# Key products of a linear-attention block on alternating halves of the array, and context products two tiles behind

## What is computed

```python
q, k, v = heads(x @ Wq), heads(x @ Wk), heads(x @ Wv)
def feature(data, proj, is_query):                 # proj: 266 x 64
    data_dash = (64 ** -0.25 * data) @ proj.T
    diag = (data * data).sum(-1) * 0.5 * 64 ** -0.5
    stab = max over features if is_query else max over everything
    return 266 ** -0.5 * (exp(data_dash - diag - stab) + 1e-4)
qp, kp = feature(q, proj, True), feature(k, proj, False)
context = einsum('nm,ne->me', kp, v)               # per head, with the sums of kp
out = (qp @ context) / (qp @ kp.sum(0))
x = x + out @ Wo + bo
```

## Time and profile before

| | |
|---|---|
| runs shown | 2225.18, 2227.09, 2228.19 us |
| median | 2227.09 us |
| the profiled execution | 2207.3 us |
| its span, first to last instruction | 2205.5 us |
| granted TensorE clock, mean over the span | 0.884 |
| TensorE busy (PE) | 1880.0 us, 85% |
| VectorE (DVE), ScalarE (ACT), GpSimd (POOL) | 1262.1, 469.0, 783.4 us |

### The profile page before, as it was taken

One profiled execution on the slowest core, in us unless ns is written; L12 is line 12 of the kernel. 1 busy time (PEld: TensorE's weight loads), 2 busy tenths in 40 slices (PEclk: granted clock), 3 DMA queues, 4 the chain that ended last, 5 costly groups with the idle time before them and its releaser, 6 DMA issues. The chain is left out here.

```text
span 2205.5 us, 22464 instructions
## 1 busy us (share of the span) xinstructions
PE 1880.0 (85%) x7734; PEld 1200.1 (54%) x7771; DVE 1262.1 (57%) x2841; ACT 469.0 (21%) x995; POOL 783.4 (36%) x688
## 2 busy tenths in 40 slices
PE   4799897777756999979969999799994999888866
PEld 4444445344442444444468887446473888765553
DVE  8666343999967999970114333426243374477523
ACT  4300214111100111111032222222112234344320
POOL 0676772666615677732021221004026101122100
PEclk8799998677767999999959999999997998977888
DMA  5232202766614666650010110101002000000002
GB/s 121 47 86 67 66 5 79 210 194 194 194 36 121 181 184 182 185 159 13 0 58 20 39 39 1 53 2 42 10 1 66 1 1 20 1 1 1 1 1 70
DMA packets 87925, 151.63 MB, mean 69 GB/s; under 512 B 37291, under 2 KB 42565, under 8 KB 87697
## 3 DMA queue, kind: packets, MB, share of 16 engines
q0 software_dynamic: 33280, 93.44, 16.3%
q1 hardware_dynamic: 54545, 56.92, 8.0%
HBM read 131.11 MB, written 19.03 MB: 68 GB/s over the span
## 5 line engine op out<-in xcount | busy, mean ns | idle before, releaser
L1110 POOL DMA_INDIRECT s_vbuf<-v_dram,s_recs x176 | 205.2, 1166 | 144.1 <-DVE s_vw L1138 74.7
L881 POOL DMA_INDIRECT s_kbuf<-k_dram,s_recs x176 | 167.3, 951 | 113.9 <-DVE s_prod L930 42.8
L1163 PE MATMUL s_pV<-s_vw,s_ohf 128*128 128x512 f32 x352 | 195.8, 638 | 0.0
L382 POOL DMA_INDIRECT rec_dram<-s_rec,s_rowid x96 | 115.7, 1205 | 93.0 <-issue 93.0
L953 PE MATMUL s_psQ<-s_qh,s_ohT 128*128 128x512 f32 x176 | 107.5, 611 | 43.4 <-DVE s_prod L930 33.1
L1157 PE MATMUL s_pA<-s_ohd,s_ohb 128*128 128x512 bf16 (+1 forms) x491 | 117.0, 343 | 7.5 <-DVE s_ohf L1136 5.1
L1138 DVE TENSOR_TENSOR s_vw<-s_vbuf,s_W 128x512 f32<-128x512 f32 x176 | 120.3, 683 | 1.7 <-DMA s_vbuf<-v_dram,s_recs 1.7
L1157 PEld LDWEIGHTS s_pA<-s_ohd,s_ohb 128*128 128x128 bf16 x528 | 50.2, 98 | 126.7 <-DVE s_ohf L1136 59.8
L1341 POOL CAST s_wh<-s_w 128x2048 fp32r<-128x2048 f32 x8 | 15.8, 1977 | 281.7 <-PE s_bank L163 157.8
L930 DVE TENSOR_TENSOR s_prod<-s_psQ,s_kbuf 128x512 f32<-128x512 f32 x176 | 112.7, 680 | 1.8 <-PE s_psQ L954 1.2
L936 DVE TENSOR_REDUCE s_W<-s_prod 128x8 f32<-128x512 f32 x176 | 111.5, 673 | 0.0
(11 more groups left out here) (423 smaller groups left out, 4212.2 us busy)
## 6 DMA issues: line engine op xcount, KB each, us to landing
s_w<-in_L_ffn_W SPq DMA_DIRECT2D x16, 512.0 KB
AT_dram<-s_A SPq DMA_DIRECT2D x10, 640.0 KB, 4.6
s_w<-in_L_mix_WqkvT SPq DMA_DIRECT2D x3, 1024.0 KB, 7.7
s_kbuf<-k_dram,s_recs POOLq DMA_INDIRECT x176, 3.8
s_vbuf<-v_dram,s_recs POOLq DMA_INDIRECT x176, 3.7
rec_dram<-s_rec,s_rowid POOLq DMA_INDIRECT x160
k_dram<-s_xn_rows SPq DMA_DIRECT2D x10, 256.0 KB, 2.2
v_dram<-s_xn_rows SPq DMA_DIRECT2D x10, 256.0 KB, 2.1
```

Source lines behind the costliest of these rows:

```text
L382: nc.gpsimd.indirect_dma_start(out=b.rec_dram, out_offset=bass.IndirectOffsetOnAxis(ap=rowid[:, t:t + 1], axis=0), in_=rec[:, t, :], in_of ...
L881: nc.gpsimd.indirect_dma_start(out=kbuf[t % KB][:, :], out_offset=None, in_=b.k_dram, in_offset=bass.IndirectOffsetOnAxis(ap=recs[:, t, 2: ...
L1110: nc.gpsimd.indirect_dma_start(out=vbuf[t % VB][:, :], out_offset=None, in_=b.v_dram, in_offset=bass.IndirectOffsetOnAxis(ap=recs[:, t, 2: ...
L1163: nc.tensor.matmul(V[:, :], ohf[i][:, :], vw[i][:, :], start=False, stop=False, skip_group_check=True).then_inc(used[i], 1)
```

## The change

The key products of two heads are made together: `dash_pair` gives head `h` partitions 0 to 63 of the array and head `h + 1` partitions 64 to 127, in turn, each with 64 rows of `kh`, `kl`, `ph`, `pl` and into a bank of its own; one semaphore increment of 2 tells of both. The maximum uses six banks instead of four. In the context passes the context matmuls of tile `t - 2` follow the key products of tile `t`; `ef` and `el` get a third buffer (`eq[n % 3]`, `el[n % 3]`, in the region of `sq`), `eh` keeps two and VectorE now waits for `used` before it overwrites one. The wait for the copied sums moves from the head of the second half to its third step. The query side is as it was.

```diff
--- before.py
+++ after.py
@@ -1698,6 +1698,7 @@
         sb("sq_reg", [P, 4 * M])
         sq = [b.over("sq_reg", f"sq{i}", [P, D], F32, i * D) for i in range(2)]
         eq = ef + [b.over("sq_reg", "ef2", [P, 4, M])]
+        el.append(b.over("sq_reg", "el2", [P, 4, M], F32R))
         diag = sb("diag", [P, 2, NT, H])
         kmax, kb, qmax, qb, den, rd = (sb(n, [P, NT, H]) for n in ("kmax", "kb", "qmax", "qb", "den", "rd"))
         g1 = sb("g1", [P, 4])
@@ -1759,6 +1760,14 @@
             c, cols = h // 2, slice(t * P, (t + 1) * P)
             return product3(nc, dst, [kh[:, c, cols]], [kl[:, c, cols]], [ph[:, h % 2, :]], [pl[:, h % 2, :]])
 
+        def dash_pair(nc, dsts, t, h):
+            c, cols = h // 2, slice(t * P, (t + 1) * P)
+            for n, (x, y) in enumerate(((kh, ph), (kl, ph), (kh, pl))):
+                for i, dst in enumerate(dsts):
+                    half = slice(i * HD, (i + 1) * HD)
+                    last = nc.tensor.matmul(dst[:, 0:M], x[half, c, cols], y[half, i, :], start=(n == 0), stop=(n == 2))
+            return last
+
         @block.tensor
         def _(pe):
             fs = Filler(pe, bank[0:4], s.fs, s.fs_free)
@@ -1796,11 +1805,11 @@
             pe.wait_ge(s.pl, 1)
             pe.wait_ge(s.kin, 1)
             pe.wait_ge(s.fs_free, fs.n)
-            km = Filler(pe, bank[0:4], s.km, s.km_free)
-            for t in range(NT):
-                for h in range(H):
-                    dst = km.take()
-                    km.done(dash3(nc, dst[:, 0:M], t, h))
+            km = Filler(pe, bank[0:6], s.km, s.km_free)
+            for t in range(NT):
+                for h in range(0, H, 2):
+                    dsts = [km.take(), km.take()]
+                    dash_pair(nc, dsts, t, h).then_inc(s.km, 2)
             pe.wait_ge(s.ones_in, 1)
             gx = Filler(pe, bank[7:8], s.gx, s.gx_free)
             pe.wait_ge(s.dg_free, 1)
@@ -1815,18 +1824,18 @@
 
             ek = Filler(pe, bank[0:4], s.ek, s.ek_free)
             for r in range(2):
-                if r:
-                    pe.wait_ge(s.ctx_in, 4)
-                for t in range(NT + 1):
+                for t in range(NT + 2):
                     if t < NT:
-                        for h in range(4):
-                            dst = ek.take()
-                            ek.done(dash3(nc, dst[:, 0:M], t, 4 * r + h))
-                    if t:
-                        u, n = t - 1, r * NT + t - 1
+                        for h in range(0, 4, 2):
+                            dsts = [ek.take(), ek.take()]
+                            dash_pair(nc, dsts, t, 4 * r + h).then_inc(s.ek, 2)
+                    if r and t == 2:
+                        pe.wait_ge(s.ctx_in, 4)
+                    if t >= 2:
+                        u, n = t - 2, r * NT + t - 2
                         pe.wait_ge(s.ekl, n + 1)
                         for h in range(4):
-                            for i, (x, y) in enumerate(((vh, eh[n % 2]), (vl, eh[n % 2]), (vh, el[n % 2]))):
+                            for i, (x, y) in enumerate(((vh, eh[n % 2]), (vl, eh[n % 2]), (vh, el[n % 3]))):
                                 last = nc.tensor.matmul(bank[4 + h][:VW, 0:M], x[:valid(u), u, 4 * r + h, :], y[:valid(u), h, :],
                                                         start=(u == 0 and i == 0), stop=(u == NT - 1 and i == 2),
                                                         skip_group_check=True)
@@ -1917,11 +1926,11 @@
             for r in range(2):
                 for t in range(NT):
                     n = r * NT + t
-                    if n >= 2:
-                        act.wait_ge(s.used, n - 1)
+                    if n >= 3:
+                        act.wait_ge(s.used, n - 2)
                     for h in range(4):
                         src = ek.take()
-                        ek.done(f(ef[n % 2][:valid(t), h, :], src[:valid(t), 0:M], ACT.Exp, bias=kb[:valid(t), t, 4 * r + h:4 * r + h + 1]))
+                        ek.done(f(eq[n % 3][:valid(t), h, :], src[:valid(t), 0:M], ACT.Exp, bias=kb[:valid(t), t, 4 * r + h:4 * r + h + 1]))
                 act.wait_ge(s.used, (r + 1) * NT)
                 for h in range(4):
                     f(cT[:VW, 4 * r + h, :], bank[4 + h][:VW, 0:M], ACT.Copy).then_inc(s.ctx_in, 1)
@@ -1990,7 +1999,7 @@
                 dve.wait_ge(s.dg_free, i)
 
             transposed(1, s.kin)
-            km = Emptier(dve, bank[0:4], s.km, s.km_free)
+            km = Emptier(dve, bank[0:6], s.km, s.km_free)
             for t in range(NT):
                 for h in range(H):
                     src = km.take()
@@ -2009,9 +2018,11 @@
             for n in range(2 * NT):
                 w = valid(n % NT)
                 dve.wait_ge(s.ek_free, 4 * n + 4)
-                v.tensor_scalar_add(eh[n % 2][:w, :, :], ef[n % 2][:w, :, :], EPS).then_inc(s.ekh, 1)
+                if n >= 2:
+                    dve.wait_ge(s.used, n - 1)
+                v.tensor_scalar_add(eh[n % 2][:w, :, :], eq[n % 3][:w, :, :], EPS).then_inc(s.ekh, 1)
                 dve.wait_ge(s.ekh, n + 1)
-                v.scalar_tensor_tensor(out=el[n % 2][:w, :, :], in0=ef[n % 2][:w, :, :], scalar=EPS,
+                v.scalar_tensor_tensor(out=el[n % 3][:w, :, :], in0=eq[n % 3][:w, :, :], scalar=EPS,
                                        in1=eh[n % 2][:w, :, :], op0=ALU.add, op1=ALU.subtract).then_inc(s.ekl, 1)
             ct = Emptier(dve, bank[0:3], s.ct_half, s.ct_free)
             for i, (_, cw) in enumerate(MC):
```

## The result

The changed kernel takes 2218.74 us, the median of 20 runs (2214.84 to 2227.08); the kernel before, 20 runs beside it, 2226.83 (2220.02 to 2231.18). The ratio is 0.9967, 95% interval 0.9957 to 0.9977: faster by a third of a per cent, about 7.4 us (5.1 to 9.6; the two medians alone lie 8.1 apart). Forecast were 2218 us, and faster by over 0.2% as the likeliest.

What follows compares the result with a forecast made beforehand. TensorE was taken to bound the maximum and both context passes, with VectorE a close second in the maximum. Maximum -1, passes -10 and clock +2 gave -9 us, carried to the median: 2218 us, range 2212 to 2228.5.

Steps and rivals of the forecast that it cites:

- The pair: Key products, maximum and passes: two matmuls on different halves run at the same time, 0.1225 us a pair, now 0.245.
- rival of queueing loads: Key products: weight loads queue, 0.216 us a pair; -1.5 us in all, 2225.6 us; chance 0.25.
- part overlap: Key products: the halves overlap partly, 0.16 us a pair; about -5.3 us, 2221.8 us; chance 0.13.
- no overlap: Key products: loads hidden but halves not simultaneous, 0.245 us a pair; +1.4 us, 2228.5 us; chance 0.08.
- exposed loads: Key products: loads no longer hidden, 0.46 us a pair; about +49 us, 2276 us; chance 0.04.
- Changes of mode: Context tiles: switching the array between halves and whole costs 0.205 and 0.15 us, 0.36 a tile; bounds 0 and 0.8.
- 80 x (0.367 - 0.354): Maximum: 80 heads go from 0.367 us to VectorE's reduction floor of 0.354, -1.0 us; bounds 0 and -1.5.
- Six banks: Maximum: two banks more only let TensorE run ahead of VectorE and bring nothing more.
- The context passes: Both passes, context two tiles behind: a tile takes 2.57 us against 2.95, together 57.2 against 67.7, taken as -10.
- Fill 5.7 as now: Start of the first half: stays 5.7 us, set by table load, exponentials and split; three key-product groups (2.2) fit inside.
- The clock: Context passes' fill and the turn: TensorE may run at 1.2 GHz there, +2 us in all, bounds 0 and +7.
- under 1.00 in the maximum: Sign to look for: a granted clock below 1.00 (2.4 GHz) in the maximum, where TensorE works 0.37 of each 0.71 us.

Runs made afterwards that it cites:

- kept_busy: Changed kernel plus matmuls of no use wherever TensorE starves (maximum, before exchange, fill, turn): 2196.70 us against 2206.46 for the kernel before.
- four_banks: Changed kernel with four banks for the maximum instead of six: 2218.57 us (one run) against 2233.53 (one run) for the kernel before.
- continuous_early: Changed kernel with both halves in one loop, tile 0's key products before the exchange, exponential table loaded early: 2210.73 us against 2225.34 for the kernel before.
- pieces_in_blocks: Changed kernel with one head's three matmuls, then the other's, instead of in turn: 2216.92 us (one run) against 2233.53 (one run) for the kernel before.

## Why the prediction was right

Its total was right, and the mechanism; some of its sizes were not, and that the total comes within 1 us is in part luck: the maximum gained 1.0 more than forecast, the passes 0.9 less, and exchange and clock cost 1.0 more. To compare them each term is taken against the profile of before on which it was made, the passes at a granted clock of 1.00 from kept_busy:

| term | forecast | measured | from |
|---|---|---|---|
| maximum | -1.0 | -2.0 | 28.99 to 27.0 |
| exchange | 0 | +0.2 | 2.27 to 2.47 |
| context passes, clock at 1.00 | -10 | -9.1 | 67.43 to 58.34 |
| clock | +2 | +2.8 | 58.34 to 61.12 |
| sum | -9 | -8.1 | 99.41 to 91.33 |

**The pair.** 0.1225 was called "an assumption all the same, and most of the risk". In the steady tile above two matmuls of a pair start 2 to 7 ns apart, their loads 3 to 9, and pairs 0.12. The Trainium skill, "TensorE: Matmul & The Clock Gate", Part 3 (Packing small matmuls), says that matmuls on different row groups start about 4 ns apart, and this trace agrees. The rival of queueing loads is refuted, and with it part overlap, no overlap and exposed loads.

**Changes of mode.** 0.36 a tile, 0.205 and 0.15; measured 0.34 by doubling them, and 0.19 and 0.14 from the starts in a steady tile.

**The maximum** was mis-sized at the term "80 x (0.367 - 0.354)". DVE was the bound, as forecast, but the floor of a reduction is 0.342. The 0.08 by which two instructions of L936 overlap isn't the overlap of these; two reductions of 0.434 overlap by 0.092. The first reductions of L1997 in the trace of before would have told it (0.345 a step); the whole of the earlier trace rows has PE's waits in it.

**Six banks** "let PE run ahead of DVE and bring nothing more": wrong. The prediction costed the PE side by its rate alone and not by the banks that a pair holds. four_banks puts them at 4.4 us of the maximum. It didn't show in the total because the change has the six.

**The context passes.** Context two tiles behind is in time, by the waits: two of them for `el`, 0.69 each where 0.8 was taken. "Fill 5.7 as now" was 6.2 in kept_busy (1785.71 to 1791.91), where `el` of tile 0 is done after 5.7 as forecast. Three groups of key products don't fit inside at will: the second and third wait for banks that ScalarE frees, and context 0 stands behind them in PE's list; here the last pair starts at 1791.14. Two useless matmuls stand behind it (1791.58), so 6.2 is an upper bound. The turn was 5.4 in the changed kernel, in part at the lower clock, forecast 5.1.

**The clock** cost what was forecast, and in the fill and at the turn, as forecast. Wrong was the sign "under 1.00 in the maximum": there it stayed at 1.00, and fell at 1806.5, behind it. kept_busy gives 2.8 as its price in the passes, within the bounds of 0 and 7; the exchange's 0.2 is gone there too (2.27), so it is 3.0 of the stretch.

**The median.** The 19.8 us "which the trace doesn't explain" are the edge scores: the stage takes 244.6 us in that profile, and 267.0 in the changed kernel's, which is one of the runs timed beside before's 2226.83. That the profile came from another chip than the timed runs is likely, but not on record. To carry microseconds or a percentage to the median gives the same here.

Not shown: why the timed gain of the stretch's later microseconds (kept_busy, continuous_early) doesn't arrive. The stage behind it varies by more than they are worth, and no run held it fixed.

## What to carry to other kernels

Where a contraction fills half of the rows, give two of them one half each; but expect the gain only once whatever consumes the products is moved far enough behind, since TensorE gets ahead of the split that it waits for. A pair takes and returns two banks at once, so count banks before pairing. And where TensorE's work in a stage becomes shorter than that of its neighbour engine, TensorE starves, and here the next stage began at the lower clock. Look at such holes before shaving matmuls: here closing the turn between the passes brought 4.1 us of the stretch, the paired matmuls 3.7.

## What the runs showed of the hardware

- Two halves of the array with 64 rows each run at full speed together, weight loads of 128 columns included: in the maximum a pair's loads start about 30 ns apart, in steady tiles the matmuls 2 to 7.
- The halves don't keep the order of the list between them: matmuls three apart in it started 9 to 14 ns apart (pieces_in_blocks).
- A change from the whole array to halves and back costs 0.34 us, by two changes more a tile; in the starts of one tile 0.19 is the way to the halves and 0.14 the way back.
- The lower clock follows the starved stage: it stayed at 1.00 while PE was busy 1.72 of 3.50 us at the end of the maximum (1803.0 to 1806.5), and was 0.50 in the 10.2 us behind it. The seven profiles with pairs in the maximum and none of the added or early work have the same 10.2 us, beginning 0.6 to 1.2 us behind the last reduction; kept_busy has none.
- The kernel before shows such stretches too, 3.4 and 6.8 us, in one profile of two, though PE is busy all through its maximum. Why only in one isn't shown.
- Reductions of 128 x 266 from PSUM, recorded with 0.434 us, follow each other every 0.342 when they wait for nothing.
- One stage, the edge scores, differs by 20 us between chips, 8% of it: 263 to 267 us on two of them, 244 to 246 on two others.
